# Experts of the last unit's first half: one multiplication of four experts by VectorE and sums by GpSimd in place of scaled adds

## What is computed

```python
x = _rmsnorm(src + sa, norm1_w)
flat = x.reshape(S, C)
shared = _swiglu(flat @ W_shared_in) @ W_shared_out
g_idx = jnp.argmax(softmax(flat @ Wg_gate + group_bias), axis=-1)          # group of 4 experts
e_probs = softmax(jnp.where(in_group, flat @ We_gate + expert_bias, -jnp.inf))
w = ...                                # top 2 of e_probs * g_prob, zero elsewhere: (S, 8)
h = _swiglu(flat @ W1_shared)
for e in range(E):
    routed = routed + h @ W2_experts[e] * w[:, e:e + 1]
out = _rmsnorm(x + shared + routed, norm2_w)
```

## Time and profile before

| | us |
|---|---|
| median of the timed runs | 834.25 |
| the profiled execution | 834.06 |
| its span, first to last instruction | 832.0 |
| TensorE busy | 804.7 (97%) |
| VectorE busy | 664.6 (80%) |
| ScalarE busy | 501.9 (60%) |
| GpSimd busy | 353.5 (42%) |
| TensorE weight loads (beside the matmuls) | 308.7 (37%) |

### The profile page before, as it was taken

The page is one execution under the profiler, slowest core; times in us unless marked ns, Lnnn a source line. Parts: engine busy times, 40 slices in busy tenths (PEclk is TensorE's granted clock), DMA queues, the critical chain, the costliest instruction groups (busy, mean ns, idle before and its releaser), DMA issues. The chain is left out here.

```text
span 832.0 us, 13459 instructions
## 1 busy us (share of the span) xinstructions
PE 804.7 (97%) x4436; PEld 308.7 (37%) x4438; DVE 664.6 (80%) x1303; ACT 501.9 (60%) x1073; POOL 353.5 (42%) x760
## 2 busy tenths in 40 slices
PE   8899999999999999999999999999999999999996
PEld 3323334334333343332323232233433434355453
DVE  6999987697789758887989999988988687673355
ACT  3267664475467627765877777777764475376441
POOL 2564328615331353424442357334253623442534
PEclk9999999999999999999999999999999999999999
DMA  4565203010200010020010323204102200000000
GB/s 119 129 168 128 81 2 78 19 58 11 70 2 2 20 62 2 9 74 3 3 51 32 78 81 83 76 14 107 37 21 58 77 2 14 1 15 2 1 13 14
DMA packets 24700, 37.83 MB, mean 45 GB/s; under 512 B 6464, under 2 KB 22080, under 8 KB 23048
## 3 DMA queue, kind: packets, MB, share of 16 engines
q1 hardware_dynamic: 24149, 36.25, 15.5%
q10 hardware_dynamic: 483, 0.74, 0.3%
HBM read 27.03 MB, written 9.11 MB: 43 GB/s over the span
## 5 line engine op out<-in xcount | busy, mean ns | idle before, releaser
L1387 ACT ACTIVATE probs<-ps 128x512 f32<-128x512 f32 x768 | 414.4, 598 | 228.0 <-PE ps L957 205.1
L1178 DVE TENSOR_REDUCE maxes<-ps 128x1 f32<-128x512 f32 x768 | 479.1, 681 | 47.6 <-PE ps L924 45.5
L924 PE MATMUL ps<-k_aug,q_aug 72*128 72x512 bf16 (+1 forms) x768 | 246.2, 382 | 3.5 <-ACT k_aug L1358 0.7
L957 PE MATMUL ps<-q_aug,k_aug 75*128 75x512 bf16 (+1 forms) x704 | 231.8, 383 | 3.3 <-DMA q_aug<-maxT 1.3
L984 PE MATMUL ps_out<-probs,v_aug 128*18 128x512 f32 x1408 | 185.4, 598 | 1.7 <-ACT probs L1387 1.0
L924 PEld LDWEIGHTS ps<-k_aug,q_aug 72*128 72x128 bf16 (+1 forms) x768 | 64.3, 96 | 162.8 <-issue 107.1
L1058 PE MATMUL ps<-w,hidden 128*128 128x512 f32 x256 | 118.7, 596 | 0.0
L957 PEld LDWEIGHTS ps<-q_aug,k_aug 75*128 75x128 bf16 (+1 forms) x704 | 59.0, 97 | 136.3 <-issue 88.9
L1279 DVE TENSOR_TENSOR prod<-ps,gate 128x512 f32<-128x512 f32 x56 | 38.7, 691 | 54.5 <-PE ps L1058 43.6
L1579 POOL TENSOR_TENSOR prod<-prod 128x512 f32<-128x512 f32 x28 | 35.5, 1268 | 85.2 <-DVE prod L1279 68.8
L1499 POOL TENSOR_SCALAR max_parts<-maxes 128x16 bf16<-128x16 f32 (+1 forms) x38 | 10.9, 288 | 141.6 <-DVE maxes L1178 141.4
(11 more groups left out here) (157 smaller groups left out, 755.3 us busy)
## 6 DMA issues: line engine op xcount, KB each, us to landing
q_aug<-qk_parts SPq DMA_DIRECT2D x7, 1152.0 KB
k_aug<-qk_parts SPq DMA_DIRECT2D x21, 384.0 KB
qk_parts<-parts SPq DMA_DIRECT2D x48, 128.0 KB, 2.3
q_aug<-qk_parts SPq DMA_DIRECT2D x11, 288.0 KB
k_aug<-qk_parts SPq DMA_DIRECT2D x27, 96.0 KB
qk_parts<-parts SPq DMA_DIRECT2D x24, 64.0 KB, 2.0
X<-in_x_dram SPq DMA_DIRECT2D x4, 256.0 KB, 4.6
w<-in_ffn_W_experts_dram SPq DMA_DIRECT2D x2, 512.0 KB, 5.8
```

What stands on the lines that cost most here:

```text
L924: pe.matmul(bank(use[i]), q_aug[p0:p1, r, at, qt * 128:(qt + 1) * 128], k_aug[p0:p1, r, at, :], start=True, stop=True).then_inc(bank_full[ ...
L957: pe.matmul(bank(use[i]), k_aug[p0:p1, r, at, kt * 128:(kt + 1) * 128], q_aug[p0:p1, r, at, :], start=True, stop=True).then_inc(bank_full[ ...
L1178: dve.tensor_reduce(maxes[:, u % 2, qt, at:at + 1], full(use[0]), AX.X, ALU.max).then_inc(bank_free[use[0][0]], 1)
L1387: act.activation(probs[:, step % P_RING, c:c + exp_run(u), :], both(use), ACT.Exp, scale=scale)\
```

## The change

The first half's experts (unit 11 in the tables) leave `VECTOR_EXPERTS`: `expert_add` goes for them, and the form of the other units is used, a multiplication of 128x512 for each bank and GpSimd's four sums for each block. The four `expert` steps are taken in the order (0,0), (0,1), (1,0), (1,1), where it was (0,0), (1,0), (0,1), (1,1). `finish` waits for GpSimd's count in place of VectorE's bank signals. The places of `router`, `shared_out`, `expert` and the first `finish` are written anew.

```diff
-VECTOR_EXPERTS = {LAST, LAST + 1}
+VECTOR_EXPERTS = {LAST + 1}
...
-           "router": [55, 55, 59, 60, 61, 63, 67, 67], "shared_out": [60], "expert": [62, 63, 67, 68],
-           "expert_add": [67, 67, 75, 75], "finish": [93, 95]}
+           "router": [52, 53, 54, 55, 56, 57, 58, 59], "shared_out": [58], "expert": [60, 61, 63, 64],
+           "finish": [90, 95]}
...
-    if u >= LAST:
+    if u in VECTOR_EXPERTS:
         steps += [(place, ("expert", u, tiles[i % 2], i // 2)) for i, place in enumerate(at["expert"])]
         steps += [(at["expert_add"][2 * half + 1], ("expert_add", u, half)) for half in range(2)]
+    else:
+        steps += [(place, ("expert", u, tiles[i // 2], i % 2)) for i, place in enumerate(at["expert"])]
+    if u >= LAST:
         return steps + [(place, ("finish", u, t)) for place, t in zip(at["finish"], tiles)]
-    steps += [(place, ("expert", u, tiles[i // 2], i % 2)) for i, place in enumerate(at["expert"])]
...
                 elif name == "finish":
                     t, = args
-                    taken(act, "expert", u, t, 1)
-                    taken(act, "shared_out", u)
+                    if u in VECTOR_EXPERTS:
+                        taken(act, "expert", u, t, 1)
+                        taken(act, "shared_out", u)
+                    else:
+                        act.wait_ge(expert_added, TT * f + t + 1)
```

## The result

The changed kernel is slower. Its timed executions have a median of 842.3 us (839.94 to 846.55, 7 runs), those of the kernel before beside them 836.63 (833.92 to 839.35, 7 runs); the ratio, estimated from all of these, is 1.008 with a 95% interval of 1.0059 to 1.0101 (that of the two medians is 1.0068). The forecast was 838.5 with a range of 836.2 to 840.8, some 0.5% slower: the direction was right, the size too small, and the measured median lies above the range. Measured again later as `z2_changed_again`, the ratio was 1.0069 (1.0043 to 1.0095). Three executions of this study, two of the kernel before (1008 and 1565 us) and one of a variant (4404 us), were far slower than all others and enter no comparison.

The account below looks back on a forecast made before the run. TensorE, busy 97% of the span, was taken as the bound. The profiled 834.06 us plus a 4.07 us shift at `x1_transpose` gave 838.13, with 0.45 for contention 838.58; forecast 838.5, range 836.2 to 840.8.

Parts of the forecast that it names:

- The stand: TensorE ahead of `shared_out`: a new wait of 2.65 us for VectorE's `mlp_up` 0 and 1, queued behind the ranking.
- The last `weigh_v`: On TensorE, delayed by the 2.65 us wait and two experts of 1.72 us each, from 802.51 to 808.60.
- `heads_transpose`: TensorE's step behind `heads_out`, forecast to start at 811.77 against 807.48, 4.29 us later.
- The two gaps of 0.5 and 0.9 us: TensorE's gaps that the experts had filled, ahead of `heads_out` and `heads_transpose`, become idle: about 0.5 and 1 us.
- VectorE beside GpSimd: `rms_apply2` 10 on VectorE is held up during GpSimd's block 1 sum; 0.45 us taken, bounds 0 and 1.03.
- The filler bound: `tail_busy` matmuls ahead of `x1_transpose` 12 end 4.64 us behind `heads_transpose`, at 816.41, a shift of 4.07 us.
- What lies behind `x1_transpose` moves along whole: From `x1_transpose` 12 to the end, no instruction or order of unit 12 changes, so the rest shifts unchanged.
- the sum, 838.5: Whole kernel: 834.06 plus 4.07 gives 838.13, with contention 838.58; forecast 838.5, slower by 4.3 us; chance 0.66.
- R4: Rival: the granted clock falls behind TensorE's stands, adding 0 to 11 us; 842 with a third of it; chance 0.08.
- R1: Rival: GpSimd's queue delays the second half's norm a further 0.5 to 2 us, 839.1 to 840.6; chance 0.14.
- R2: Rival: no wait at `shared_out`, only the experts' move; `x1_transpose` 1.42 us later, 835.5; chance 0.07.
- R3: Rival: not slower; other work fills the experts' gaps, `heads_out` stays at 805.33, 0.22 us gained, 833.8; chance 0.05.

Follow-up runs that it names:

- z2_changed_again: The changed kernel as it is, measured once more for a second profile; median 841.97 us, ratio 1.0069.
- x1: Changed kernel with the router's places written so that VectorE's ranking stands behind `mlp_up` 0 and 1 again; median 837.87 us, ratio 1.0038.
- x2: Kernel before with only the changed kernel's `router` and `shared_out` places; scaled adds and experts' places stay; median 842.45 us, ratio 1.0076.
- x3_fill: Changed kernel with 11 unused matmuls put where TensorE stands ahead of `shared_out`; median 840.12 us, ratio 1.0072.
- y1: Changed kernel with the 11 filler matmuls, and unit 10's second norm and `unit_out` moved ahead of the first half's experts; median 842.25 us, ratio 1.0085.
- y3: Changed kernel with 5 filler matmuls ahead of `shared_out` in place of 11; median 841.65 us, ratio 1.0065.
- z1: Changed kernel with ranking behind `mlp_up` 0 and 1, unit 10's second norm early, `expert` (1,1) at place 67; median 837.35 us, ratio 1.0022.

## Why the prediction was right in part and wrong in the size

- The stand: forecast 2.65 us, with `shared_out` 6.12 us behind the mark; measured 2.51 and 6.15. Right in cause and size, and shown by x1 (gone) and x2 (alone).
- The last `weigh_v`: forecast 6.09 us later, measured without the clock 6.25 (x3_fill). `heads_transpose`: forecast 4.29, measured 4.41. The two gaps of 0.5 and 0.9 us came as forecast. Right, low by 0.1.
- VectorE beside GpSimd: forecast to bring the shift to 4.52 us at `x1_transpose`; measured 4.72, of which 0.46 is the contention and `unit_out` in the queue by y1, where I had taken 0.45 for the contention. Right as far as the two can be told apart. The filler bound that I gave for the case without it, 4.64 us behind `heads_transpose`, was 4.70.
- What lies behind `x1_transpose` moves along whole: right in the runs without a fall (10.44 to 10.45 us to the adds in before, x1, x2 and x3).
- So the sum, 838.5, describes the order well: 834.06 + 4.73 = 838.8, and x3_fill's median is 4.8 us over that of the kernel before.
- The step that failed is the granted clock, which the sum puts at nothing, in the change and in the kernel before. For the change it is R4: I gave it 0.08, because one stand of 2.4 us in the earlier trace rows had left the clock at 1.00, and a single case at the very start of the run carried the whole argument. Near the end the clock fell with a stand of 2.4 to 2.9 us in all five profiles that have one there. What it adds on the mean can be taken from all timed executions: 15 of the changed kernel, mean 842.4 us at a mean granted clock of 0.9933; 64 of the kernel before in the four later sets of measurements, mean 835.8 at 0.9956. Among those of before, each us at the 1.2 GHz level goes with 0.43 us of time (a line through the 64, with that time worked out as twice the missing share of the clock times the span). By it 4.9 us of the 6.6 between the means are there at equal clock, the order, and 1.7 go with the lower clock. That these 1.7 come from the stand alone isn't shown, since x1_rank_back has nearly the same mean clock without it.
- For the kernel before, I read it as if its clock never fell. Its profile has a fall at 35 to 38 us (windows of 0.79, 0.50, 0.85), the changed kernel's profile one at 54 to 61, from a part that the change doesn't touch. The spread of the kernel before, 833.4 to 840.6 us, goes with it: the 13 of the 64 executions with a clock of 0.998 or more have a mean of 834.2, the four with 0.990 one of 840.5. With 3 runs I took 834.25 for its median, where 7 gave 836.63 and the 64 give 835.4. The range left no room for either.
- Added up, from 838.5 to the changed kernel's mean of 842.4: 1.7 for the base (835.8 against the 834.06 of the sum), 0.5 for the order (4.9 against 4.4), 1.7 for the clock. R4's price, 842 with a third of the bound, lies near the measured median by luck: it stood on the low base and asked of the clock twice what it gave.
- R1 wasn't needed, R2 is what x1_rank_back shows (1.42 forecast at `x1_transpose` without contention, 2.01 measured with it), R3 stayed out.

Open: what decides whether a stand or a row of short ones lets the clock fall. Near the end, 2.5 us ahead of `shared_out` did in 3 of 3 profiles, 2.4 to 2.9 us ahead of `x1_transpose` in 2 of 2, 1.21 us there did once, 1.41 us ahead of `shared_out` didn't; the row of 0.5, 0.9 and 0.3 us did in 3 profiles (changed, again, y3) and didn't in 2 (x1, x3). The stand at the start that I had leaned on is in every profile, and there length and fall don't go together: with 1.9 to 2.5 us it left the clock at 1.00 in 8 of 8, with 1.3 to 1.6 us the clock fell some 1 us behind it in 2 of 4 (x3, z1). Timelines of TensorE, the kernel before, then x3_fill with a window:

```profile
8.73 0.66 PE L864 MATMUL ps<-ident,src 128*128 128x128 f32 x4 [2.41 <-DVE src L1126]
```

```profile
8.83 0.66 PE L866 MATMUL ps<-ident,src 128*128 128x128 f32 x4 [1.45 <-DVE src L1133]
```

```profile
10.00:12.00 2.00, 1.95 (x4) 0.83 (x3) 0.95 (x5) 0.12 (x1) 0.00 (x0) 0.51 0.00 0
```

So the length of one stand doesn't decide it, at the start or near the end.

## What to carry to other kernels

When a step is moved in an order that all engines share, list every instruction that it issues on each engine and what it now stands in front of: here 14 small instructions of VectorE, moved two places up, cost more than the saving that the change was built on. An engine's saved time is worth nothing where that engine waits anyway; and matmuls that fill a gap of the bounding engine are free where they lie and cost time once they are moved ahead of the gap: here 3.44 us of experts cost 1.69. On a kernel bound by TensorE price a new stand both with and without the clock's fall behind it (1.6 to 1.7 us where the fall lasted 3.4 us, 3.2 where it lasted 6.8), and put neither at nothing by one precedent, which may lie in another part of the run. And read the granted clock of the kernel before in several executions, not in one, before its time is taken as the base.

## What the hardware showed that I had not expected

- VectorE's multiplications of the norms (two tensors read, all in SBUF) wait for GpSimd's running instruction and end some 0.15 us behind it: 128x128, 0.34 us alone, took up to 1.38 us in the kernel before (two of them 1.64), four of them 2.21 and 2.98 us for 1.13, two 1.61 for 0.61. GpSimd's 128x512 never took more than 1.28 us. VectorE's multiplication of a PSUM bank (0.69 us) wasn't lengthened beside a sum, nor were its small ranking instructions (0.16 to 0.17 us, changed kernel, 797.5 to 798.3) beside GpSimd's of 0.20. The Trainium skill, page GPSIMD Engine Reference, § 1, names the shared interface; which side waits, and how long, these rows show.
- A stand of 2.5 us was followed by the 1.2 GHz level in all three profiles that have it ahead of `shared_out`: once the clock fell before the stand was over (801.4, the stand ended at 801.8), twice 1.2 us behind it (x2, z2), and it stayed there 3.4 to 6.8 us although TensorE was busy again. The Trainium skill, page TensorE: Matmul & The Clock Gate, Part 1, has idleness as the cause; the late stands agree with it, and so do the same stands filled with matmuls (1.00 in x3 and y1), while the stands of 1.9 to 2.5 us at the start don't.
- The same program's clock falls at different places early in the run from one execution to the next (changed kernel: 54 to 61 us in one profile, 35 to 38 in the other), and its time with it.
